# A fused embedding, attention and mixture-of-experts layer on one core: three experts in flight, all products on VectorE, routing weights folded in as square roots

## The chip, the core and the metric

The kernel runs on one core of one Trainium2 chip. The core has five engines with an instruction stream each: TensorE (PE), VectorE (DVE), ScalarE (ACT), GpSimd (POOL) and SyncE (SP, which only issues transfers). They wait for one another by semaphores. The metric is the device time of one execution in microseconds (us), as a median of several runs.

## What is computed

Token ids of shape 8 x 1024 pick rows of 256 numbers from a table. Then comes one layer, here cut to what matters:

```
h = table[x]                                         # 8 x 1024 x 256
n = layernorm(h)
q, k, v = n @ Wqkv + b          # 16 heads of 16; attention runs over the 8 rows of a column
h = h + softmax(q k^T / 4) v @ Wo + bo
n = layernorm(h)
s = sigmoid(n @ Wg)                                  # 16 experts in 4 groups
cw = top-4 experts within the 2 best groups, chosen by s + bias;  cw = 2.5 * s / sum(s)
h = h + relu(n @ Ws1)^2 @ Ws2 + sum_e cw[e] * relu(n @ W1[e])^2 @ W2[e]
```

## The kernel before

The 1024 columns are cut into B = 16 blocks of 64 columns, so a block has T = 512 tokens. All weights lie in SBUF as a high and a low part (`_hi`, `_lo`, the low part being what rounding to fp32r left over), and each product is three matmuls: high x high, high x low, low x high. So each activation that TensorE reads is also split in two: a rounded copy and a difference.

**The expert steps.** Each block has 18 steps (X_ALL): two halves of the shared expert and 16 routed experts. A step is `up` (6 matmuls of 512 columns into `psH`), an activation chain, and `down` (12 matmuls of 256 columns, added up in `psY`). The chain for a routed expert is: ScalarE takes relu of `psH` into `r_sb` (L497) and squares it (L499); VectorE multiplies by the broadcast routing weight `cwB` into `p_sb` (`weigh`, L641); ScalarE rounds `p_sb` to `hid_hi` (L510); VectorE subtracts to get `hid_lo` (`hidden_lo`, L647). `up` runs two experts ahead of `down`, and `psH`, `r_sb`, `p_sb` and `hid` have two buffers each. At the end of a block VectorE adds `psY` to `h` (`add_experts`, L653).

**The stages around them.** Attention, normalisation and routing of the following blocks are laid into these steps by tables of half steps h = 0 to 35. While block b's experts run, `attention(b+1, h)` and `head(b+2, h)` do one piece each at fixed h, before and after the expert's own instruction. `head` holds the first normalisation, its transposes (`k_sb` to `psB`), q, k and v, and the first product. `attention` holds the products q x k (`product`, L279, eight per block, four of them on GpSimd and four on VectorE, into the four slots of `ring`), their sum over heads by matmul (`score`, L940), softmax, spreading of the probabilities (L956), the weighted values on VectorE (L684, eight per block), their sums over positions (`position_sum`, L300 to L305, six on GpSimd and two on VectorE; the result goes to `q_sb`), the output projection (L966), second normalisation (`v_sb`), transposes, logits (L978), and the routing on VectorE (L707 to L758, five pieces). `rstd_of` on GpSimd gives 1/sqrt(variance) from the statistics of L659, and VectorE applies it (`normalise`, L666). The routing weights are transposed on TensorE, stored to DRAM and read back spread over all partitions (`cwB`).

**What sets the order.** Each engine runs its instructions in the order in which they stand; nothing is moved by a scheduler. Block 0's stages and part of block 1's run first, then a hardware loop runs seven times over two blocks, and the last two blocks stand in straight code. Weights are loaded and split in the meantime of block 0's stages.

## Time and profile before

| | |
|---|---|
| median of 3 runs | 1469.57 us (1466.58 to 1469.63) |
| span of the profiled execution | 1464.6 us |
| busy: TensorE, VectorE | 1267.7 us (87%), 1189.9 us (81%) |
| busy: GpSimd, ScalarE | 689.5 us (47%), 679.8 us (46%) |
| chain that ended last | VectorE 39%, TensorE 31%, issue 19%, others 11% |

The busy time of TensorE counts pipelined matmuls to their modelled ends, so a high share doesn't mean that it runs at its peak. The span is cut by the recurring work: VectorE's addition at L653 closes each of the 16 blocks, and the distance of two such rows is the time of a block in the middle of the run. "issue" in the chain is time for which the profile shows no wait.

### The profile page before, as it was taken

The page shows a single profiled execution, that of the slowest core. Times are in us where ns is not written, and L with a number is a line of the kernel's source. Part 1 is how long each engine was busy: PE and PEld are TensorE (multiplying, and loading weights), DVE is VectorE, ACT ScalarE, POOL GpSimd, SP SyncE. Part 2 cuts the span into 40 slices and gives each one's busy share as a digit, 9 for nine tenths or more (in the row PEclk, how much of TensorE's full clock was granted, in tenths as well). Part 3 has the DMA queues.
Part 4 walks back from the last instruction along what each step waited for, and adds up shares of the span by engine and source line. Part 5 has one row for each costly group of instructions (what it writes and reads, how often), then busy time and mean ns, then how long its engine had stood idle before and what let it go on. Part 6 is the DMA issues. An engine that isn't in the chain of part 4 may idle for free.

```text
span 1464.6 us, 22940 instructions
## 1 busy us (share of the span) xinstructions
PE 1267.7 (87%) x7488; PEld 1033.1 (71%) x7488; DVE 1189.9 (81%) x1792; ACT 679.8 (46%) x1138; POOL 689.5 (47%) x753
## 2 busy tenths in 40 slices
PE   4458898889888899888989889898988989989898
PEld 2146767768677687767778677776867768677787
DVE  3868889697987969789797888969798797978854
ACT  2234444544444454444544444454553445445355
POOL 7744535365263635535464363536526363442600
PEclk9579999999999999999999999999999999999999
DMA  2302111111211112111111212112121111212122
GB/s 66 125 16 74 58 60 58 61 62 55 73 62 57 58 44 88 58 61 58 66 65 44 78 67 62 58 46 73 58 73 58 61 58 44 88 44 73 59 73 73
DMA packets 33748, 92.21 MB, mean 63 GB/s; under 512 B 4800, under 2 KB 13376, under 8 KB 33600
## 3 DMA queue, kind: packets, MB, share of 16 engines
q1 hardware_dynamic: 30528, 81.99, 16.7%
q0 software_dynamic: 3072, 8.39, 2.0%
q8 instruction: 75, 1.23, 0.4%
q14 instruction: 73, 0.60, 0.1%
HBM read 81.46 MB, written 8.91 MB: 62 GB/s over the span
## 4 chain that ended last, share of the span: by engine, by line
DVE 39%; PE 31%; issue 19%; POOL 5%; ACT 5%; DMA 1%; DVEq 1%; ACTq 0%; POOLq 0%; SPq 0%
PE psY L900 9%; PE psH L887 8%; DVE ring L684 7%; PE psB L927 5%; DVE p_sb L641 5%; DVE hid_lo L647 5%; PE psA L966 3%; DVE g_gt L723 2%; DVE ring L300 2%; PE psA L978 2%; DVE ring L302 2%; DVE ring L279 1%; DVE k_sb L666 1%; ACT hid_hi L510 1%; DVE stats L659 1%
## 5 line engine op out<-in xcount | busy, mean ns | idle before, releaser
L900 PE MATMUL psY<-w_hi,hid_hi 128*128 128x256 f32 x1152 | 339.0, 294 | 53.6 <-DVE hid_lo L647 50.3
L510 ACT CAST hid_hi<-p_sb 128x512 fp32r<-128x512 f32 x256 | 159.2, 622 | 388.8 <-DVE p_sb L641 379.5
L900 PE MATMUL psY<-w_lo,hid_hi 128*128 128x256 f32 x1152 | 330.5, 287 | 0.0
L900 PE MATMUL psY<-w_hi,hid_lo 128*128 128x256 f32 x1152 | 330.2, 287 | 0.0
L279 POOL TENSOR_TENSOR ring<-q_sb,k_sb 128x1024 f32<-128x1024 f32 x64 | 169.1, 2653 | 309.1 <-PE psA L940 205.2
L900 PEld LDWEIGHTS psY<-w_hi,hid_hi 128*128 128x128 f32 x1152 | 223.6, 194 | 107.4 <-DVE hid_lo L647 72.6
L647 DVE TENSOR_TENSOR hid_lo<-p_sb,hid_hi 128x512 fp32r<-128x512 f32 x256 | 214.6, 838 | 93.4 <-ACT hid_hi L510 73.7
L887 PE MATMUL psH<-xT_hi,w_hi 128*128 128x512 f32 x576 | 235.6, 409 | 10.9 <-issue 8.7
L641 DVE TENSOR_TENSOR p_sb<-r_sb,cwB 128x512 f32<-128x512 f32 x256 | 214.2, 837 | 34.1 <-ACT r_sb L499 27.2
L900 PEld LDWEIGHTS psY<-w_lo,hid_hi 128*128 128x128 f32 x1152 | 224.6, 195 | 9.8
L887 PE MATMUL psH<-xT_lo,w_hi 128*128 128x512 f32 x576 | 230.2, 400 | 0.0
L887 PE MATMUL psH<-xT_hi,w_lo 128*128 128x512 f32 x576 | 229.8, 399 | 0.0
L900 PEld LDWEIGHTS psY<-w_hi,hid_lo 128*128 128x128 f32 x1152 | 224.6, 195 | 0.0
L300 POOL TENSOR_TENSOR ring<-ring 128x512 f32<-128x512 f32 x96 | 146.8, 1529 | 135.8 <-DVE ring L684 134.3
L497 ACT ACTIVATE r_sb<-psH 128x512 f32<-128x512 f32 x288 | 171.2, 594 | 57.2 <-PE psH L887 44.2
L499 ACT ACTIVATE r_sb<-r_sb 128x512 f32<-128x512 f32 x288 | 182.6, 634 | 9.1
L887 PEld LDWEIGHTS psH<-xT_hi,w_hi 128*128 128x128 f32 x576 | 111.0, 193 | 54.6 <-issue 23.1
L887 PEld LDWEIGHTS psH<-xT_hi,w_lo 128*128 128x128 f32 x576 | 109.9, 191 | 26.0
L887 PEld LDWEIGHTS psH<-xT_lo,w_hi 128*128 128x128 f32 x576 | 110.8, 192 | 16.9
L399 POOL TENSOR_TENSOR mv<-stats 128x4 f32<-128x4 f32 x32 | 20.3, 635 | 197.0 <-DVE stats L659 197.0
L302 POOL TENSOR_TENSOR ring<-ring 128x256 f32<-128x256 f32 x96 | 104.1, 1085 | 7.5
L279 DVE TENSOR_TENSOR ring<-q_sb,k_sb 128x1024 f32<-128x1024 f32 x64 | 89.6, 1401 | 21.5 <-issue 9.3
(133 smaller groups left out, 2137.5 us busy)
## 6 DMA issues: line engine op xcount, KB each, us to landing
cwB<-cw_dram SPq DMA_DIRECT2D x128, 512.0 KB, 3.7
out<-h SPq DMA_DIRECT2D x32, 256.0 KB, 5.4
p_sb<-w_t SPq DMA_DIRECT2D x3, 512.0 KB
cwB<-w_t SPq DMA_DIRECT2D x3, 512.0 KB, 4.5
h<-w_t SPq DMA_DIRECT2D x2, 512.0 KB
xin<-table,idx_now POOLq DMA_INDIRECT x56
cwB<-wqkv_t SPq DMA_DIRECT2D x2, 384.0 KB, 3.2
cw_dram<-cwT SPq DMA_DIRECT2D x16, 32.0 KB, 1.6
```

What stands on the lines that cost most here:

```text
L279: ns.tensor_tensor(ring[:, t % 4, :, :].rearrange("p l (m n) -> p l m n", m=L), qv.unsqueeze(2).to_broadcast([P, 2, L, NN]), kv.unsqueeze( ...
L300: ns.tensor_tensor(a[:, :, 0:4, :], a[:, :, 0:4, :], a[:, :, 4:8, :], ALU.add).then_inc(sum_step[who], 1)
L302: ns.tensor_tensor(a[:, :, 0:2, :], a[:, :, 0:2, :], a[:, :, 2:4, :], ALU.add).then_inc(sum_step[who], 1)
L497: nc.scalar.activation(r_sb[:, e % 2, :], psH[:, e % 2, :], ACT.Relu).then_inc(relu_done, 1)
L499: nc.scalar.activation(r_sb[:, e % 2, :], r_sb[:, e % 2, :], ACT.Square).then_inc(sq_done, 1)
L510: nc.scalar.copy(hid[0][:, e % 2, :], src[:, e % 2, :]).then_inc(hid_hi, 1)
L641: nc.vector.tensor_tensor(p_sb[:, e % 2, :], r_sb[:, e % 2, :], cwB[:, (r // QN) % 2, r % QN, :], ALU.mult).then_inc(p_ready, 1)
L647: nc.vector.tensor_tensor(hid[1][:, e % 2, :], src[:, e % 2, :], hid[0][:, e % 2, :].bitcast(f32), ALU.subtract).then_inc(hid_lo, 1)
L684: nc.vector.tensor_tensor(ring[:, t % 4, :, :], ps[:, :, :], v_sb[:, ih, :].unsqueeze(1).to_broadcast([P, 2, T]), ALU.mult).then_inc(av_re ...
L887: last = nc.tensor.matmul(psH[:, e % 2, :], W1[a][:, kh, e, :], x[b][:, kh, :], start=(kh == 0 and (a, b) == PASSES[0]), stop=(kh == KH - ...
L900: last = nc.tensor.matmul(psY[:, j // 2, (j % 2) * D:(j % 2 + 1) * D], hid[a][:, e % 2, j * P:(j + 1) * P], W2[b][:, e, :], start=(e == 0 ...
L927: last = nc.tensor.matmul(psB[:, n % 2, :], WQKV[a][:, kh, 2 * c + ih, :], xT1[b][:, kh, :], start=(kh == 0 and (a, b) == PASSES[0]), stop ...
```

## The change

- **Experts.** `up` runs three experts ahead (AHEAD), `hid` has three buffers (R). The routing weight is applied as its square root ahead of the square: VectorE does `max(psH, 0) * cwB` in one instruction from PSUM into `r_sb`, ScalarE squares twice, once as fp32 into `p_sb` and once rounded into `hid_hi`, VectorE subtracts. The shared halves keep the relu on ScalarE. `weigh` works two experts ahead of `down`'s step and `hidden_lo` one, so no engine needs another's result of the same step.
- **Products.** All eight are on VectorE.
- **Attention's output** goes to a tile of its own, `o_sb`; its split parts go to `xT2` in place of `xT1`, the second normalisation's result to `o_sb` in place of `v_sb`, and scores go to `psB` in place of `psA`.
- **Normalisation** is applied on ScalarE (identity with scale and bias from `rstd` and a new `nmr`, which GpSimd computes with one more operation).
- **Root of the weights.** ScalarE computes `exp(-0.5 * ln(1 + exp(-x)))`, GpSimd the power -0.5 of the sum; VectorE multiplies them. Loads of activation tables are placed when the program is built (the last order below shows them).
- **Order.** The stages of a block stand at positions p = 0 to 71 in one table. While block b's experts run, positions 36 to 71 of block b+1 and 0 to 35 of block b+2 are laid in. All products, scores and softmax and the first two weighted values now lie below 36. There is no hardware loop; everything stands in straight code, with constants in the waits.
- **Start.** Weights come in other pieces through eight staging areas; the first q, k, v matmuls wait for all of GpSimd's constants (`CONST_ALL`).

```
-        hid = [sb(f"hid_{p}", [P, 2, T], f32r) for p in ("hi", "lo")]
+        hid = [sb(f"hid_{p}", [P, R, T], f32r) for p in ("hi", "lo")]
...
-            def relu_square(blk, e):
...
-                nc.scalar.activation(r_sb[:, e % 2, :], psH[:, e % 2, :], ACT.Relu).then_inc(relu_done, 1)
-                nc.scalar.activation(r_sb[:, e % 2, :], r_sb[:, e % 2, :], ACT.Square).then_inc(sq_done, 1)
...
-            def hidden_hi(blk, e):
...
-                nc.scalar.copy(hid[0][:, e % 2, :], src[:, e % 2, :]).then_inc(hid_hi, 1)
...
+            def square(n):
...
+                if e < SH:
+                    nc.scalar.activation(r_sb[:, n % 2, :], psH[:, n % 2, :], ACT.Relu).then_inc(relu_done, 1)
...
+                nc.scalar.activation(p_sb[:, n % 2, :], r_sb[:, n % 2, :], ACT.Square)
+                wait(act, w2_mm, n - R + 1)
+                nc.scalar.activation(hid[0][:, n % R, :], r_sb[:, n % 2, :], ACT.Square).then_inc(hid_hi, 1)
...
-                nc.vector.tensor_tensor(p_sb[:, e % 2, :], r_sb[:, e % 2, :],
-                                        cwB[:, (r // QN) % 2, r % QN, :], ALU.mult).then_inc(p_ready, 1)
+                nc.vector.scalar_tensor_tensor(r_sb[:, n % 2, :], psH[:, n % 2, :], 0.0, cwB[:, (r // QN) % 2, r % QN, :],
+                                               ALU.max, ALU.mult).then_inc(weighed, 1)
...
+                    act.wait_ge(sigexp_ready, nth(blk, 1, 1))
+                    nc.scalar.activation(lgt[:, :, :], sig[:, :, :], ACT.Ln, bias=1.0).then_inc(log_ready, 1)
+                    act.wait_ge(log_ready, nth(blk, 1, 1))
+                    nc.scalar.activation(lgt[:, :, :], lgt[:, :, :], ACT.Exp, scale=-0.5).then_inc(root_ready, 1)
...
+            def root_of_sum(blk):
...
+                nc.gpsimd.tensor_tensor(w_rec[:, :], w_sum[:, :], half_neg[:, :], ALU.pow).then_inc(sum_root_ready, 1)
...
-            def main(blk, nxt, far):
-                for t in (5, 7):
-                    product(pool, nc.gpsimd, blk, t)
...
+        SCORES = [20, 23, 27, 29]
+        SPREADS = [34, 34, 36, 37, 39, 39, 41, 42]
+        V_PRODUCTS = [14, 16, 18, 19, 22, 22, 25, 27]
...
             def step_of(blk, e):
+                n = blk * X_ALL + e + AHEAD
+                if n < B * X_ALL:
+                    up(n)
+                stage_of(blk + 1, HALF + 2 * e)
+                stage_of(blk + 2, 2 * e)
+                down(blk, e)
+                stage_of(blk + 1, HALF + 2 * e + 1)
+                stage_of(blk + 2, 2 * e + 1)
```

The order on VectorE around the softmax, in a block in the middle of the run. Before (L641 is `weigh`, L647 `hidden_lo`, L684 a weighted value; REGISTER_ALU rows are the loop's arithmetic for waits):

```order
L772 TENSOR_TENSOR s_sb<-psA,s_max 128x512
L641 TENSOR_TENSOR p_sb<-r_sb,cwB 128x512
L777 TENSOR_REDUCE s_sum<-s_sb 128x64
...
L788 TENSOR_TENSOR probs<-s_sb,probs 64x512 x2
...
L666 TENSOR_SCALAR k_sb<-xin,mv,rstd 128x256 x4
L638 REGISTER_ALU
L641 TENSOR_TENSOR p_sb<-r_sb,cwB 128x512
L680 REGISTER_ALU
L684 TENSOR_TENSOR ring<-psB,v_sb 128x1024
```

The same place after (L663 is `hidden_lo`, L692 a weighted value):

```order
L789 TENSOR_REDUCE s_max<-psB 128x64
L792 TENSOR_TENSOR s_sb<-psB,s_max 128x512
L797 TENSOR_REDUCE s_sum<-s_sb 128x64
L799 RECIPROCAL s_rec<-s_sum 128x64
L801 TENSOR_TENSOR s_sb<-s_sb,s_rec 128x512
L663 TENSOR_TENSOR hid_lo<-p_sb,hid_hi 128x512 x2
L808 TENSOR_TENSOR probs<-s_sb,probs 64x512 x2
L692 TENSOR_TENSOR ring<-psB,v_sb 128x1024
L692 TENSOR_TENSOR ring<-psA,v_sb 128x1024
```

The `weigh` between the subtraction of the maximum and the sum is gone, and so are the normalisation and the `weigh` between the probabilities and the first weighted value.

The order on VectorE in the routing, after (L658 is `weigh`, L300 a product, L732 to L768 are routing):

```order
L727 TENSOR_REDUCE gsc<-pairs 128x16
L658 SCALAR_TENSOR_TENSOR r_sb<-psH,cwB 128x512
L663 TENSOR_TENSOR hid_lo<-p_sb,hid_hi 128x512
L732 TENSOR_TENSOR g_gt<-gsc 128x64
...
L736 TENSOR_REDUCE g_rank<-g_gt 128x16
L300 TENSOR_TENSOR ring<-q_sb,k_sb 128x1024 x2
...
L763 TENSOR_SCALAR w_sum<-w_sum 128x4
L766 TENSOR_TENSOR cw<-lgt,e_gt 128x64
L768 SCALAR_TENSOR_TENSOR cw<-cw,w_rec 128x64
L300 TENSOR_TENSOR ring<-q_sb,k_sb 128x1024
```

Products stand between the pieces of the routing, and between L763 and L768 lies the power on GpSimd that L768 waits for.

The order on ScalarE at the logits, after (L522 and L524 are the two squares, L593 copies the logits, L596 to L600 are the three functions):

```order
L593 COPY lg<-psA 128x128
L596 ACTIVATE sig<-lgt 128x64
L598 ACT_TABLE_LOAD
L598 ACTIVATE lgt<-sig 128x64
L600 ACT_TABLE_LOAD
L600 ACTIVATE lgt<-lgt 128x64
L522 ACTIVATE p_sb<-r_sb 128x512
L524 ACTIVATE hid_hi<-r_sb 128x512
```

Each block has two loads of activation tables ahead of the next expert's squares; before, the whole program has one, at its start.

## Rows read from the trace of the kernel before

**Rows 1.** Two blocks: us, then busy (count) of PE, PEld, DVE, ACT, POOL; clock, DMA

```profile
637.00:726.00 89.00, 79.88 (x471) 65.03 (x471) 74.28 (x112) 42.22 (x72) 42.94 (x46) 0.96 0.19 61
726.00:811.50 85.50, 77.33 (x467) 63.55 (x465) 73.58 (x113) 40.91 (x69) 42.71 (x46) 0.98 0.18 63
```

**Rows 2.** VectorE's timeline (start, duration), the additions that close blocks

```profile
200.60 1.22 DVE L653 TENSOR_TENSOR h<-psY,h 128x1024 f32<-128x1024 f32 x1
...
811.48 1.22 DVE L653 TENSOR_TENSOR h<-psY,h 128x1024 f32<-128x1024 f32 x1
...
1332.51 1.22 DVE L653 TENSOR_TENSOR h<-psY,h 128x1024 f32<-128x1024 f32 x1
...
1409.47 1.22 DVE L653 TENSOR_TENSOR h<-psY,h 128x1024 f32<-128x1024 f32 x1
...
1458.99 1.23 DVE L653 TENSOR_TENSOR h<-psY,h 128x1024 f32<-128x1024 f32 x1 [1.79 <-PE psY L900]
```

**Rows 3.** The chain that ended last, one block: start us, us, what

```profile
707.66 1.69 PE psA L978 x16
...
775.40 2.87 PE psA L966 x24
778.27 1.40 PE psH L887 x6
779.67 1.42 PE psY L900 x12
...
793.21 1.69 PE psA L978 x16
```

**Rows 4.** VectorE's timeline in the same block, wait ahead in brackets

```profile
712.82 1.87 DVE L641 TENSOR_TENSOR p_sb<-r_sb,cwB 128x512 f32<-128x512 f32 x1 [0.73 <-ACT r_sb L499]
714.61 2.42 DVE L723 TENSOR_TENSOR g_gt<-gsc 128x64 f32<-128x64 f32 x1
...
728.30 2.89 DVE L647 TENSOR_TENSOR hid_lo<-r_sb,hid_hi 128x512 fp32r<-128x512 f32 x1
...
733.61 2.11 DVE L647 TENSOR_TENSOR hid_lo<-p_sb,hid_hi 128x512 fp32r<-128x512 f32 x1 [0.69 <-ACT hid_hi L510]
...
748.51 0.69 DVE L641 TENSOR_TENSOR p_sb<-r_sb,cwB 128x512 f32<-128x512 f32 x1
749.11 1.22 DVE L684 TENSOR_TENSOR ring<-psB,v_sb 128x1024 f32<-128x1024 f32 x1
...
774.17 0.68 DVE L800 TENSOR_TENSOR xT_lo<-q_sb,xT_hi 128x512 fp32r<-128x512 f32 x1
```

**Rows 5.** GpSimd's timeline in the same block

```profile
711.74 5.21 POOL L279 TENSOR_TENSOR ring<-q_sb,k_sb 128x1024 f32<-128x1024 f32 x2 [6.59 <-ACT k_sb L528]
...
738.86 0.57 POOL L399 TENSOR_TENSOR mv<-stats 128x4 f32<-128x4 f32 x1 [3.68 <-DVE stats L659]
...
741.72 1.05 POOL L411 TENSOR_TENSOR rstd<-mv,half_neg 128x4 f32<-128x4 f32 x1
750.41 1.30 POOL L300 TENSOR_TENSOR ring<-ring 128x512 f32<-128x512 f32 x1 [7.65 <-DVE ring L684]
...
769.60 0.52 POOL L305 TENSOR_TENSOR q_sb<-ring 128x128 f32<-128x128 f32 x1
```

**Rows 6.** Groups by line and form: xcount, busy us, mean ns, idle before

```profile
L499 ACT ACTIVATE r_sb<-r_sb 128x512 f32<-128x512 f32 x288 | 182.6, 634 | 9.1
...
L491 ACT ACT_TABLE_LOAD x1 | 1.3, 1283 | 0.9 <-PEq L1084 0.9
...
L491 ACT CAST w_hi<-cwB 128x256 fp32r<-128x256 f32 x2 | 0.8, 404 | 0.0
```

**Rows 7.** Waits in the block of 89.0 us: total, times, longest

```profile
PEld psH L887 <- issue: 3.1, 2, 2.3
```

**Rows 8.** GpSimd's timeline at the start, its last constant

```profile
26.99 0.91 POOL L467 TENSOR_SCALAR_AFFINE_SELECT not_first<-not_first 128x64 f32<-128x64 f32 x1
```

**Rows 9.** The chain at the start: block 0's second transposed split

```profile
97.35 1.15 DVE xT_lo L673
```

More of the change, by code:

```diff
@@ L122, in lm_tower_layer @@
         rstd = [sb(f"rstd{w}", [P, TT]) for w in range(2)]
+        nmr = [sb(f"nmr{w}", [P, TT]) for w in range(2)]
         lg = sb("lg", [P, TT, 2, E])
@@ L160, in lm_tower_layer @@
         small_in = sem("small_in")
-        w_in = [sem(f"w_in{k}") for k in range(STAGES)]
+        w_in = [sem(f"w_in{k}") for k in range(14)]
         w_hi = sem("w_hi")
@@ new lines, in normalise @@
+            def normalise(w, blk, src, dst):
+                act.wait_ge(ln_rstd[w], nth(blk, 1, 1))
+                if w == 0:
+                    wait(act, prod_ready[1], nth(blk, LP, 0))
+                d = dst[:, :, :].rearrange("p a t -> p (a t)").rearrange("p (j d) -> p j d", d=D)
+                for j in range(TT):
+                    last = nc.scalar.activation(d[:, j, :], src[:, j, :], ACT.Identity,
+                                                bias=nmr[w][:, j:j + 1], scale=rstd[w][:, j:j + 1])
+                last.then_inc(xn_ready[w], 1)
@@ L613, in _ @@
-            with act.Fori(0, B // 2 - 1) as i:
-                block_act((i, 0), (i, 1), (i, 2))
-                block_act((i, 1), (i, 2), (i, 3))
-            block_act((None, B - 2), (None, B - 1), None)
-            block_act((None, B - 1), None, None)
+            for p in range(HALF):
+                stage_of(0, p)
+                if p == A_T1 + 2:
+                    act.wait_ge(const_step, CONST_ALL)
+                    nc.scalar.copy(spread[:, :, :].rearrange("p a b -> p (a b)"),
+                                   rows(r_sb[:, :, :])).then_inc(spread_ready, 1)
@@ L833, in block_dve @@
-            def block_dve(blk, att, nxt):
-                for e in range(X_ALL):
-                    if e + 1 < X_ALL:
-                        weigh(blk, e + 1)
-                    for h, last in ((2 * e, False), (2 * e + 1, True)):
-                        if att is not None:
-                            attention(att, h)
-                        if nxt is not None:
-                            head(nxt, h)
-                        if last:
-                            break
-                        if e + 1 < X_ALL:
-                            hidden_lo(blk, e + 1)
-                        elif att is not None:
-                            hidden_lo(att, 0)
-                add_experts(blk)
@@ L850, in _, with step_of @@
-            for h in range(V_T1):
-                head((None, 0), h)
-            for k in range(PIECES_QKV):
+            def step_of(blk, e):
+                n = blk * X_ALL + e
+                if n + 2 < B * X_ALL:
+                    weigh(n + 2)
+                if n + 1 < B * X_ALL:
+                    hidden_lo(n + 1)
+                if e == 0 and blk > 0:
+                    add_experts(blk - 1)
+                for k in range(PIECES_ATT, PIECES_ALL):
+                    if n == LO_AT[k - PIECES_ATT] - HALF:
+                        weight_lo(k)
+                for h in (2 * e, 2 * e + 1):
+                    stage_of(blk + 1, HALF + h)
+                    stage_of(blk + 2, h)
```

655 lines of the change are left out of this document (332 added, 323 removed).

## The prediction

> **What bounds the kernel now.** I read the shares of busy time first: TensorE 87%, VectorE 81%, both too high for either to be idle for long and too low for either to be the limit everywhere. So I cut the run into blocks. The additions that close a block stand 200.60 to 1332.51 us, 13 blocks apart [rows 2], 87.1 us each; the last but one takes 77.0 us (1332.51 to 1409.47) and the last 49.5. About 1208 of the 1465 us are blocks 1 to 14, so the block in the middle decides.
>
> In a block of 85.5 us TensorE is busy for 77.3 and VectorE for 73.6 [rows 1]. The chain tells which of them sets the time. From one logits' end (707.66 + 1.69 = 709.35) to the next (793.21 + 1.69 = 794.90) is 85.5 us [rows 3]. In its second part, from the start of the output projection at 775.40 to 794.90, the chain is TensorE without a gap: 19.5 us. In its first part, 709.35 to the end of the last split of attention's output at 774.17 + 0.68 = 774.85 [rows 4], it runs over VectorE: 65.5 us, and 0.55 to hand over. So the block is a ring of two parts: **65.5 us of VectorE, then 19.5 us of TensorE**. I split the first again at the end of the first weighted value (749.11 + 1.22 = 750.33) [rows 4]: 41.0 us of routing, products and softmax, and 24.5 us of weighted values and position sums. In the latter GpSimd works without a gap from 750.41 to 769.60 + 0.52 = 770.12 [rows 5].
>
> Two more things cost time. First, VectorE's instructions with both inputs in SBUF stretch whenever GpSimd runs: a subtraction that takes 0.69 takes 2.89 and 2.11, a comparison of 64 elements 2.42 [rows 4], in the shadow of a 2.6 us product [rows 5]; the ones from PSUM (L684, 1.22) do not. The Trainium skill's "SBUF — State Buffer", Who interferes with whom, says that the pair of ports shared by VectorE and GpSimd is an exclusive lock; by that rule, these rows agree. Second, the longer block (89.0 against 85.5 us, [rows 1]) has 3.1 us in which TensorE waited for nothing that is shown [rows 7], and 0.02 less clock. Blocks alternate in this way, so I take it as the edge of the loop, one per two blocks. The Trainium skill, "Runtime: NRT & Kernel Launch", Instruction fetch mechanics, says that a taken branch outside the fetched window costs a fetch; the row fits it, but does not show the fetch.
>
> **The first 41.0 us, term by term.** Start-to-start distances count, not durations: a `weigh` occupies VectorE for 749.11 - 748.51 = 0.60 us [rows 4].
> - GpSimd's products go: their shadow goes with them: 1.87 - 0.69, 2.42 - 0.22, 2.89 - 0.69 and 2.11 - 0.69 [rows 4] are 7.0 us less. This stretch had four products on VectorE, and has four after (positions 22, 22, 25, 27); the other four now lie at 14 to 19, in the part that TensorE fills. A product is 1.13 us start to start, as L684 with the same 1024 elements.
> - The normalisation of the next block moves to ScalarE: 1.3 us less (4 of 0.41, overlapped). There it costs 4 of 0.40 [rows 6].
> - Two waits for `hid_hi` within a step, 0.69 each [rows 4], go, since no step needs a result of its own: 1.4 less.
> - Two `weigh` and one `hidden_lo` fewer, 1.8 less. The block's closing addition and the first statistics now follow the first weighted value: 2.5 less here (and they lie beside GpSimd's sums there).
> - **Added:** the exponential is no longer covered by a `weigh`: 0.65 and two hand-overs, 0.8 more. Its cover was the instruction between L772 and L777.
> - The power on GpSimd takes 1.05 [rows 5] and replaces a reciprocal of 0.18, with hand-overs and one more product 1.2 more. Nothing covers it: behind the wait stand a product and two expert steps. GpSimd could be late there, but its queue holds only the bias addition ahead.
> - The probabilities' split is followed at once by the values that need them spread: 0.75 more (its cover was the normalisation).
> - **Two table loads per block**, 1.28 each [rows 6], with Ln and a second exponential: ScalarE stands for 3.3 us at the logits. The squares of one expert wait behind them, and VectorE's `hidden_lo` for them: in order, route part 1 takes VectorE 1.8 and the next `weigh` 0.6, so 5.4 - 3.4 = 2.0 us more.
>
> Sum: 41.0 - 7.0 - 1.3 - 1.4 - 1.8 - 2.5 + 0.8 + 1.2 + 0.75 + 2.0 = **31.7 us**; I take 31.
>
> `weigh` now reads PSUM, and no row has this form. Bounds: 0.60 as before, or below (a gain of 0.1) if its reads escape GpSimd as L684 does, to 0.7 if clamping costs something; by 11 of them 1 us at most. I take 0.60.
>
> **The 24.5 us of sums.** The sums stay six on GpSimd (19.7 us, [rows 5]) and two on VectorE. Now the next block's variance root stands between them in GpSimd's order, 738.86 to 742.77, 3.9 us [rows 5]. GpSimd then needs 23.6, and the copy and split of the output 1.5 more: 25.1. VectorE alone needs about the same: six steps of 1.2, seven values of 1.13, two sums of 1.95, closing addition and statistics 2.4, 21.4 in all, and up to 3 of locking. **25.1 us.** If the root were late, statistics of step 1 delay it and all sums behind it: up to 3 us more.
>
> **The TensorE part.** From projection to logits it now has all six q, k, v groups instead of three: 2.87 + 6 x 1.40 + up and down (1.40 and 1.42, three and two of them) + transposes 0.87 + logits 1.69 = **20.9 us** [rows 3]. VectorE and the root for the second normalisation fit beside it (2.7 + 4 + 1.3 of 12.7 us).
>
> Block: 31 + 25.1 + 0.5 + 20.9 = **77.5 us**, and no loop edge. TensorE's own work is the same: 77.3 us busy, of which ends of matmuls that waited are part; I put it at 74 to 76. So TensorE is about to be the limit as well.
>
> ScalarE, at 42 us of 85.5 [rows 1], loses one 0.63 operation [rows 6] for each of 16 experts and gains 1.3 x 2 + 3.1: 37.
>
> **Start and end.** Block 0's chain: q, k, v now wait for GpSimd's last constant at 26.99 + 0.91 = 27.9 [rows 8] and not 20.6, 7 us later; its eight products on VectorE win that back (9 against 16 us), and eight staging areas some 3 us: the transposed split ends at 95 in place of 97.35 + 1.15 = 98.5 [rows 9]. Then logits 3.5 and the 31 us stretch, with 11 expert instructions less (-6.6), five weight splits (+5.6) and the second value: the first period starts at about **127 us**. Fourteen full periods follow, then a block without the head of another: 77.5 less q, k, v, transposes and scores (14.2) is **63.3**. The last: 18 `down` and 15 `up` (46.6), the closing addition 1.2 and 5.6 to the span's end: **53.4**, as before's last block already runs at TensorE's pace.
>
> Sum: 127 + 14 x 77.5 + 63.3 + 53.4 = 1328.7 us of span. The median before lies 5.0 above the span shown (1469.57 - 1464.6), so **1334 us**.
>
> **The rivals.**
> - *TensorE is the limit.* If the sums on GpSimd and the waits of ScalarE are covered, a block is TensorE's own 75.5: 14 x 2 less, **1306 us**. For it: two engines within 3 us of each other. Against: TensorE has to wait for the split output once a block.
> - *The table load costs more than its row.* The one row (1.28) stands at the start, with nothing ahead of it. If ScalarE must also run empty, a switch costs about double, VectorE's `hidden_lo` waits 2.7 longer: 14 x 2.7, **1372 us**. The Trainium skill, "ScalarE: Activation LUTs", What ACT_TABLE_LOAD costs, has 1283 ns and a drain of 1380 ns. By its section Table sets one set holds both exp and ln; the built order has two loads a block all the same, so that rule gives nothing here.
> - *The sums stretch.* GpSimd and VectorE each have 22 to 25 us there, and lock one another out; 5 us more a block, **1404 us**. For it: in the same stretch before, subtractions already stretch.
> - *Slower than before.* VectorE is in order, and each of its waits then stops the expert chain: q, k, v at position 16 (3.2), the transposes at 55 (2), tables 2, exponential, power and spreading 2.7, beside its own 71 and 8 of locking, is 88.9 us. It decides from 87.3 us a block on. 14 x 11.4 more: **1494 us**. Against: half of these waits lie in the part that TensorE fills.
>
> **How the numbers follow.** Forecast 0.50 (1320 to 1355 on its own), TensorE as the limit 0.16, tables 0.11, sums 0.16, slower 0.05; the remaining 0.02 no change. The range for 8 in 10 goes from the one rival to the other, 1300 to 1405. 0.2% is about what a measurement of this kernel can tell from no change: faster 0.93, same 0.02, slower 0.05.
>
> **What would show it.** Closing additions 77 to 78 us apart and all alike, without alternation; no stretched comparison in the routing; on ScalarE two table loads of 1.28 a block with one `hidden_lo` waiting about 2 us; TensorE waiting 2 to 3 us a block at the output projection; a first closing addition at about 206 us. I am wrong if the blocks still alternate, if a `weigh` from PSUM takes clearly more than 0.7, or if GpSimd's sums take more than 25 us from the first value.

## The result and the profile after

The changed kernel takes **1339.39 us** (median of 4 runs, 1338.98 to 1341.05); the kernel before, on the same chip, 1469.6 (1466.58 to 1470.88). The ratio is 0.9124, 95% interval 0.9103 to 0.9145. The prediction was 1334 us (1300 to 1405), faster.

The page after: TensorE's share of busy time has risen from 87% to 92%, VectorE's is 80% (81% before), ScalarE's 47% (46%), GpSimd's 39% (47%).

```profile
PE 1228.9 (92%) x7488; PEld 1020.1 (76%) x7488; DVE 1067.7 (80%) x1726; ACT 630.1 (47%) x1072; POOL 524.8 (39%) x723
...
DVE 45%; PE 28%; ACT 10%; issue 10%; POOL 4%; DVEq 2%; DMA 1%; ACTq 0%; POOLq 0%; SPq 0%
```

The second line is the chain that ended last, by engine. It gives VectorE 45%, and it misleads, as will be seen. VectorE's timeline has the additions that close blocks (L669 now), and answers to [rows 2]:

```profile
215.26 1.21 DVE L669 TENSOR_TENSOR h<-psY,h 128x1024 f32<-128x1024 f32 x1
...
602.54 1.21 DVE L669 TENSOR_TENSOR h<-psY,h 128x1024 f32<-128x1024 f32 x1
...
680.01 1.21 DVE L669 TENSOR_TENSOR h<-psY,h 128x1024 f32<-128x1024 f32 x1
...
1222.36 1.21 DVE L669 TENSOR_TENSOR h<-psY,h 128x1024 f32<-128x1024 f32 x1
1287.14 1.23 DVE L669 TENSOR_TENSOR h<-psY,h 128x1024 f32<-128x1024 f32 x1
1333.90 1.22 DVE L669 TENSOR_TENSOR h<-psY,h 128x1024 f32<-128x1024 f32 x1 [2.90 <-PE psY L905]
```

The first and the fourteenth are 13 blocks and 1007.1 us apart: 77.47 a block, where [rows 2] give 87.1. The one shown is 77.47 too; the alternation of [rows 1] is gone. One block in the windows view, whole and in two parts (columns as in [rows 1]):

```profile
602.54:680.01 77.47, 75.28 (x468) 62.98 (x468) 65.76 (x108) 38.32 (x67) 32.38 (x45) 1.00 0.22 69
...
626.23:667.87 41.64, 41.64 (x265) 33.75 (x265) 32.23 (x65) 21.04 (x38) 12.60 (x16) 1.00 0.16 51
667.87:703.70 35.83, 33.65 (x206) 29.24 (x205) 33.53 (x44) 17.29 (x31) 19.79 (x28) 1.00 0.27 90
```

The first part goes from the output projection to the end of the last scores. **TensorE is busy for all of its 41.64 us.** In the second, up to the next projection, it waits 2.2 us, in three places:

```profile
PE psY L905 <- DVE h L669: 1.5, 1, 1.5
PE psA L973 <- DVE xT_lo L820: 0.4, 1, 0.4
PE psB L963 <- DVE probs L808: 0.3, 1, 0.3
```

So a change to another engine can save TensorE 2.2 us of waiting a block, and little else. (It isn't a strict bound: busy time counts matmuls to their modelled ends, and a later run took 0.44 us off it as well.) The granted clock has changed too: it is 1.00 here, and was 0.96 and 0.98 in [rows 1], where about the same matmuls were busy for 79.88 and 77.33 us in place of 75.28. VectorE at the logits, in the same block (start, duration; it answers to the first rows of [rows 4]):

```profile
650.30 0.69 DVE L658 SCALAR_TENSOR_TENSOR r_sb<-psH,cwB 128x512 f32<-128x512 f32 x1 [0.29 <-PE psH L890]
652.42 0.69 DVE L663 TENSOR_TENSOR hid_lo<-p_sb,hid_hi 128x512 fp32r<-128x512 f32 x1 [1.42 <-ACT hid_hi L524]
653.03 0.22 DVE L732 TENSOR_TENSOR g_gt<-gsc 128x64 f32<-128x64 f32 x1
...
664.29 0.23 DVE L768 SCALAR_TENSOR_TENSOR cw<-cw,w_rec 128x64 f32<-128x64 f32 x1 [1.09 <-POOL w_rec L444]
...
668.08 0.68 DVE L789 TENSOR_REDUCE s_max<-psB 128x64 f32<-128x512 f32 x1
```

The comparison of 64 elements is back from 2.42 to 0.22. The two waits which the prediction charged to the block, for the table loads (1.42) and for the power (1.09), are there in size. The scores end at 667.87 on TensorE, and VectorE takes them up at 668.08: both engines arrive within 0.2 us of each other. What these waits cost is therefore open in this trace, and the first experiments test it.

### The profile page after: what moved, and what is told of

The parts are those of the page before. It is cut to its first block, busy times and chain, and to the rows that moved or that the text cites. A ratio compares the mean times of both kernels' runs of the same rounds, so it can differ in the third digit from the quotient of the medians.

```text
span 1339.3 us, 19873 instructions
## 1 busy us (share of the span) xinstructions
PE 1228.9 (92%) x7488; PEld 1020.1 (76%) x7488; DVE 1067.7 (80%) x1726; ACT 630.1 (47%) x1072; POOL 524.8 (39%) x723
## 4 chain that ended last, share of the span: by engine, by line
DVE 45%; PE 28%; ACT 10%; issue 10%; POOL 4%; DVEq 2%; DMA 1%; ACTq 0%; POOLq 0%; SPq 0%
DVE hid_lo L663 10%; PE psB L932 8%; DVE ring L692 7%; PE psY L905 7%; PE psH L890 6%; DVE r_sb L658 6%; DVE ring L300 4%; PE psA L973 4%; DVEq L741 2%; DVE ring L320 2%; ACT p_sb L522 2%; DVE o_sb L327 2%; DVE stats L675 2%; ACT hid_hi L524 2%; ACT L598 1%
## 5 line engine op out<-in xcount | busy, mean ns | idle before, releaser
L522 ACT ACTIVATE p_sb<-r_sb 128x512 f32<-128x512 f32 x288 | 180.9, 628 | 346.8 <-DVE r_sb L658 345.7
L663 DVE TENSOR_TENSOR hid_lo<-p_sb,hid_hi 128x512 fp32r<-128x512 f32 x288 | 232.7, 812 | 27.2 <-ACT hid_hi L524 26.8
L320 POOL TENSOR_TENSOR ring<-ring 128x512 f32<-128x512 f32 x96 | 126.6, 1318 | 239.6 <-DVE ring L692 239.6
L300 DVE TENSOR_TENSOR ring<-q_sb,k_sb 128x1024 f32<-128x1024 f32 x128 | 160.0, 1263 | 70.1 <-ACT k_sb L552 69.6
L658 DVE SCALAR_TENSOR_TENSOR r_sb<-psH,cwB 128x512 f32<-128x512 f32 x256 | 174.2, 681 | 30.7 <-PE psH L890 30.6
L524 ACT ACTIVATE hid_hi<-r_sb 128x512 fp32r<-128x512 f32 x288 | 178.2, 619 | 9.5 <-PE psY L905 8.5
L444 POOL TENSOR_TENSOR w_rec<-w_sum,half_neg 128x4 f32<-128x4 f32 x16 | 16.6, 1040 | 289.8 <-DVE w_sum L763 289.8
L692 DVE TENSOR_TENSOR ring<-psB,v_sb 128x1024 f32<-128x1024 f32 x64 | 77.7, 1214 | 14.3 <-PE psB L963 14.3
L932 PE MATMUL psB<-xT_hi,wqkv_hi 128*128 128x512 f32 x192 | 79.3, 413 | 8.0 <-POOL not_first L493 8.0
L322 POOL TENSOR_TENSOR ring<-ring 128x256 f32<-128x256 f32 x96 | 81.9, 853 | 7.5
```

What stands on the lines that cost most here:

```text
L300: ns.tensor_tensor(ring[:, t % 4, :, :].rearrange("p l (m n) -> p l m n", m=L), qv.unsqueeze(2).to_broadcast([P, 2, L, NN]), kv.unsqueeze( ...
L320: ns.tensor_tensor(a[:, :, 0:4, :], a[:, :, 0:4, :], a[:, :, 4:8, :], ALU.add).then_inc(sum_step[who], 1)
L322: ns.tensor_tensor(a[:, :, 0:2, :], a[:, :, 0:2, :], a[:, :, 2:4, :], ALU.add).then_inc(sum_step[who], 1)
L522: nc.scalar.activation(p_sb[:, n % 2, :], r_sb[:, n % 2, :], ACT.Square)
L524: nc.scalar.activation(hid[0][:, n % R, :], r_sb[:, n % 2, :], ACT.Square).then_inc(hid_hi, 1)
L658: nc.vector.scalar_tensor_tensor(r_sb[:, n % 2, :], psH[:, n % 2, :], 0.0, cwB[:, (r // QN) % 2, r % QN, :], ALU.max, ALU.mult).then_inc(w ...
```

## The experiments

Each changed kernel ran in four executions beside the kernel before (1467.5 to 1469.7 us in the four sets). The median is a blunt measure for edits of a few microseconds, since the last block but one comes out in different lengths. In it TensorE waits 3.2 us for `o_sb`, and what follows runs for a longer or a shorter while at the lower level of its clock. Here is that block in the changed kernel and in one of the kernels below (the one with both moves and the later wait; windows):

```profile
1222.36:1287.14 64.78, 60.09 (x381) 54.18 (x382) 46.50 (x87) 29.81 (x53) 19.05 (x27) 0.97 0.22 74
```

```profile
1200.72:1269.48 68.76, 64.15 (x381) 57.91 (x382) 46.49 (x87) 30.25 (x53) 19.06 (x27) 0.90 0.22 70
```

The same 381 matmuls take 4.1 us more at a granted clock of 0.90. The block is 68.6 to 68.9 us long in the profiled executions without the logarithm, with the early statistics, with the early root and with both moves, 67.2 with the power covered, and 64.5 to 65.6 in those with the later wait alone and with the addition in halves. So the distance of closing additions in the middle is the measure of an edit, and up to 4 us of a median are not the edit's.

### The logarithm and its table loads, left out

```
-                    nc.scalar.activation(lgt[:, :, :], sig[:, :, :], ACT.Ln, bias=1.0).then_inc(log_ready, 1)
+                    nc.scalar.activation(lgt[:, :, :], sig[:, :, :], ACT.Identity).then_inc(log_ready, 1)
```

> The changed kernel with the logarithm replaced by an identity, which leaves out part of the computation: the routing weights are then not the root of the sigmoid. Both table loads of each block go with it. Theory: the loads cost what hid_lo waits behind them in the trace, 1.4 us a block, up to the 2.0 us of my sum: 14 to 16 blocks, 1309 to 1319 us. Rival A (each load also drains the engine): 4 us or more a block, below 1285 us. Rival B (TensorE is the limit already and takes the gain): within 5 us of 1339.

Measured: 1341.17 us (1340.26 to 1342.07), ratio 0.9128. VectorE there, at the same places:

```profile
647.24 0.68 DVE L663 TENSOR_TENSOR hid_lo<-p_sb,hid_hi 128x512 fp32r<-128x512 f32 x1
...
664.30 0.69 DVE L789 TENSOR_REDUCE s_max<-psB 128x64 f32<-128x512 f32 x1 [1.25 <-PE psB L945]
```

The wait of 1.42 is gone, and one of 1.25 for the scores has come 17 us later. Blocks take 77.36 us, 0.1 less. (The profiled execution begins 3.2 us sooner and loses 3.8 in the last block but one.) **The loads cost nothing where they stand**, since TensorE has the time of that stretch.

### The wait for the power, covered

```
-        ROUTE_FIRST = [0, 1, 8, 13, 16, 21, 27]
+        ROUTE_FIRST = [0, 1, 8, 13, 16, 21, 26, 27]
...
-        V_ROUTE = [56, 57, 58, 61, 63, 63]
+        V_ROUTE = [56, 57, 58, 61, 63, 63, 64]
```

> The changed kernel, with the last operation of the routing (the one that waits about 1.1 us a block for the power on GpSimd) one half step later, so that a product and an expert step stand in between; nothing else is moved. The prediction charged this wait to every block (1.2 us, nothing covers it). Theory A: it is on the path, and 1.1 us a block come off: 1322 to 1326 us. Theory B: it lies where TensorE is the limit (output projection to the last scores), VectorE's wait for the last scores grows by as much, and nothing moves: 1336 to 1342 us.

Measured: 1339.62 us (1337.56 to 1342.14). The wait is gone from the row, and the same trade appears:

```profile
661.83 0.22 DVE L769 SCALAR_TENSOR_TENSOR cw<-cw,w_rec 128x64 f32<-128x64 f32 x1
664.24 0.69 DVE L790 TENSOR_REDUCE s_max<-psB 128x64 f32<-128x512 f32 x1 [0.99 <-PE psB L946]
```

A block takes 77.37 us, again 0.1 less, and theory B holds. Together the two show that in the routing stretch, 31 us in the prediction, taking away one of VectorE's waits buys nothing. It doesn't follow that adding to it is free, which the next run tests.

### Products on GpSimd again

```
+                for t in (1, 3, 5, 7):
+                    if p == V_PRODUCTS[t]:
+                        product(pool, nc.gpsimd, blk, t)
...
-                    if p == V_PRODUCTS[t]:
+                    if p == V_PRODUCTS[t] and t % 2 == 0:
```

> The changed kernel, with products 1, 3, 5 and 7 (positions 16, 19, 22 and 27) on GpSimd again, as before; the tables and all else stay. It undoes the one part to which the prediction gave its largest term, 7.0 us a block. Theory A, the prediction's own: a block's routing stretch is VectorE's, so four shadows of GpSimd stretch its subtractions and comparisons again, less four products of 1.13 that it no longer does: 7.0 - 4.5 = 2.5 to 7 us a block, and a product of 2.6 instead of 1.13 ahead of the last scores 1.5 more. By 14 to 15 blocks: 1380 to 1440 us. Theory B, from the run without the logarithm: from the output projection to the last scores TensorE is the limit (41.7 us of a block) and VectorE has about 1.3 us to spare at the end of it, so most of this is covered: 0 to 2 us a block, 1340 to 1370 us.

Measured: 1394.17 us (1391.4 to 1395.4), 55 more than the changed kernel. That is theory A's range, not B's. A block takes 80.48 us, 3.0 more, and 11 us come once, at the start (first closing addition at 226.08; the edit also lets GpSimd wait there until the weights are split, since `ring` holds them). GpSimd and VectorE at the same moment:

```profile
682.86 2.41 POOL L300 TENSOR_TENSOR ring<-q_sb,k_sb 128x1024 f32<-128x1024 f32 x1 [3.00 <-PE psB L949]
685.22 2.86 POOL L439 TENSOR_TENSOR xin<-xin,bo_sb 128x1024 f32<-128x1024 f32 x1
```

```profile
683.22 2.60 DVE L667 TENSOR_TENSOR hid_lo<-p_sb,hid_hi 128x512 fp32r<-128x512 f32 x1
685.74 2.42 DVE L743 SCALAR_TENSOR_TENSOR cho<-g_rank,cho 128x64 f32<-128x64 f32 x1
```

A subtraction that takes 0.68 alone ends 0.55 us after GpSimd's product, and an operation of 0.22 ends 0.08 us after GpSimd's bias addition. That addition was there before; in the changed kernel it runs at 643.06, ahead of the routing, and the products in front of it in GpSimd's order push it into the routing. VectorE is busy 67.06 us a block in place of 65.76 though it has four products fewer: 1.3 + 4 x 1.13 = 5.8 us of stretching. VectorE had no slack against this in the changed kernel, where it took up the scores 0.2 us after they were there, and 3.0 us reach the end of the block. They are seen on TensorE: its waits in the block are 4.9 us in place of 2.2, the new ones for `weigh` (1.2), for the routing weights (1.0) and for the probabilities (0.8 in place of 0.3). So TensorE isn't busy for all of the first part any more. This is the largest part of the change that a single run isolates.

### From the other side: the old kernel without its loop, then without GpSimd's products

The loop written out on all engines:

```
-            with pe.Fori(0, B // 2 - 1) as i:
+            for i in range(B // 2 - 1):
```

> The kernel before, with its seven passes of the hardware loop written out as straight code; nothing else differs. My theory: the alternation of block lengths (89.0 and 85.5 us) is the loop's edge, 2 to 3.5 us each, so 7 edges go: 1446 to 1456 us, ratio to before 0.984 to 0.990, and all blocks in the middle near 85.5 us. Rival: the alternation comes from something else with a period of two blocks (buffers alternate too), and the time stays at 1470 us with blocks that still alternate.

Measured: 1445.3 us (1442.35 to 1447.97), ratio 0.9839 (0.9789 to 0.9888). Two blocks far apart are now alike (windows view):

```profile
200.86:286.01 85.15, 77.81 (x470) 64.17 (x469) 73.37 (x112) 41.39 (x71) 42.73 (x46) 0.98 0.20 63
626.62:711.77 85.15, 77.91 (x470) 64.24 (x469) 73.37 (x113) 41.40 (x71) 42.73 (x46) 0.98 0.20 63
```

The loop's seven passes cost 23.5 us, 3.4 each (16 to 31 us by the interval, 2.4 to 4.4 a pass). Then, on top of it, the odd products on VectorE, behind the even ones:

```
-                for t in (5, 7):
-                    product(pool, nc.gpsimd, blk, t)
...
+                    product(dve, nc.vector, blk, 2 * V_PRODUCTS.index(h) + 1)
```

> The kernel before in straight code, and all eight products on VectorE, each odd one right behind the even one before it. To be compared with the same kernel without that move. My theory, by the terms of the sum: GpSimd's lock takes 7.0 us a block from VectorE's part of the ring, and four more products of 1.13 us add 4.5 there: 2.5 us less a block, some 37 us less in 15 blocks, 1410 to 1420 us. Rival: VectorE is the engine that decides and only gets more work: 4.5 us more a block, 1515 us.

Measured: 1421.96 us (1419.09 to 1424.21), 23 less than with the loop written out alone. The direction is right, the size a miss, and the trace tells where: the first closing addition comes at 189.35 in place of 200.86, and a block is 84.29 instead of 85.15. So 11.5 us are won once at the start and only 0.9 a block. The block, to be held against the two above:

```profile
612.23:696.52 84.29, 77.86 (x470) 64.19 (x469) 71.00 (x116) 41.30 (x71) 32.15 (x42) 0.98 0.20 63
```

VectorE is busy 2.4 us less (71.00 for 73.37), close to the 7.0 - 4.5 = 2.5 that the shadows less four products of 1.13 give, and the block is shorter by 0.9. The waits say where the rest went. TensorE's wait for the routing weights fell from 1.2 to 0.2 us, while its waits for `hid_lo` (3.1, now 3.2) and for the values (2.5) stayed. VectorE for its part now waits 3.1 us for ScalarE's `r_sb` in place of 1.3.

### Two experts in flight in the new order

```
-    R = 3
-    AHEAD = 3
+    R = 2
+    AHEAD = 2
...
-            up(2)
```

> The changed kernel with two experts in flight instead of three (R and AHEAD 2); the order of all other work is the same. My sum had no term for the depth as such, only for the waits within a step that go. Theory: with two, the second square of an expert waits for down of the expert before the last, so VectorE can't run ahead of TensorE; where it does now, it waits: 2 to 5 us more a block, 1370 to 1415 us. Rival: the depth is not what brought the gain (the order is), and the time stays within 5 us of 1339.

Measured: 1705.68 us (1704.54 to 1707.24), ratio 1.1608. A clear miss, by over 290 us. One block is 102.35 us (windows), and the waits in it say why:

```profile
645.75:748.10 102.35, 84.62 (x468) 69.05 (x468) 64.01 (x109) 39.33 (x67) 31.89 (x45) 0.92 0.16 52
```

```profile
DVE r_sb L658 <- PE psH L890: 32.4, 10, 9.1
...
ACT hid_hi L524 <- PE psY L905: 18.9, 5, 8.6
...
PE psA L985 <- DVE xT_lo L681: 3.7, 1, 3.7
```

`weigh` works two experts ahead, and with two in flight that is the expert whose `up` TensorE has in hand in the same step. VectorE waits 32.4 us a block for it, its products and splits queue up behind, and TensorE waits for those (the last row is the longest of its waits; it is idle for 17.7 us of the block). The wait that was expected, the second square behind `down`, is there too (18.9 us on ScalarE); the one for `up` wasn't foreseen. The new order is only good with `up` three ahead. The edit takes away the lead and the third `hid` buffer together, so what each is worth is open, and so is what they would be worth in the old order, which had two of both with its steps dealt out otherwise; that was not run.

### The start

```
-                if p == A_T1 + 2:
+                if p == A_QKV[-1] + 1:
...
-            pe.wait_ge(const_step, CONST_ALL)
...
+                if p == SCORES[0]:
+                    pe.wait_ge(const_step, CONST_ALL)
```

> The changed kernel, with TensorE's wait for all of GpSimd's constants ahead of the first scores (position 20) instead of the first q, k, v, and the copy of one of these constants on ScalarE behind q, k, v of block 0. It tests what the start costs, once. q, k, v of block 0 start at 32.04 us in the changed kernel, the constants end at 31.95, while the split of the normalised rows is there some us earlier. If this wait is what delays the start, the first closing addition comes 4 to 10 us earlier (205 to 211 in place of 215.26) and the time is 1329 to 1335 us. If the loads of weights through eight staging areas set the start (the rows of block 0 land at 13 instead of 9 us, the weights after them), less than 3 us: 1336 to 1340. Blocks stay at 77.4 us in both.

Measured: 1335.13 us (1333.38 to 1336.63), 4.3 less. q, k, v of block 0 begin at 26.50 us and not at 32.04. The first addition stands at 208.01, but kernels whose start is unchanged have it at 215.26, 211.98 and 212.10, so by the traces 4 to 7 us can be the effect; the medians and the run with both moves below give 4 to 5.

### The stretch of the sums

First the statistics of the next block's first normalisation, from behind the first value to position 21 of the block before:

```
-                if p == V_STATS1:
-                    dve.wait_ge(xin_in[par], 64 * (blk // 2 + 1))
-                    norm_stats(0, blk, xin[par])
+                for at, nb in ((V_STATS1, 0), (21, blk + 1)):
+                    if p == at and nb < B and (p == 21 or blk == 0):
+                        dve.wait_ge(xin_in[nb % 2], 64 * (nb // 2 + 1))
+                        norm_stats(0, nb, xin[nb % 2])
```

> The changed kernel, with the first statistics of the next block (two instructions on VectorE, 1.3 us in all, from the same rows of x) at position 21 of the block before, among the products, instead of behind the first weighted value; the variance root on GpSimd stays where it was, between the position sums. Theory B: a block is a ring of TensorE from the output projection to the last scores (41.7 us) and VectorE from there to the output's split (35.8 us). 1.3 us of VectorE leave the second part, but GpSimd, which the root and six sums keep busy there, sets its end as well: the gain is 0 to 1.3 us a block, 1320 to 1339 us. If GpSimd's queue alone sets that part, nothing moves: 1338 to 1341.

Measured: 1330.75 us (1328.04 to 1333.36); 76.57 us a block, 0.9 less. TensorE's busy time in a block falls by 0.44 of it (75.28 to 74.84), and of its waits the 0.4 us at the output projection is gone. Thirteen blocks would give 11.7 us; the median fell by 8.6, since the last block but one is 4.1 longer. Then GpSimd's root as well:

```
-                if p == P_RSTD1 and blk > 0:
-                    rstd_of(0, blk)
+                if p == 28 and blk + 1 < B:
+                    rstd_of(0, blk + 1)
```

> The changed kernel, with both the first statistics (position 21 of the block before, VectorE) and the variance root that follows from them (position 28 of the block before, GpSimd, 4 operations, 3.9 us) moved ahead of the softmax. It takes 3.9 us of GpSimd and 1.3 us of VectorE out of the stretch of the sums, which the prediction made 25.1 us long because of GpSimd (19.7 for the sums, 3.9 for the root, 1.5 for the copy and split). The prediction's step: that stretch becomes 19.7 + 1.5 = 21.2 by GpSimd, but VectorE needs some 22.5 itself, so 1.3 to 2.6 us a block come off: 1303 to 1321 us. Rival: VectorE alone sets the stretch, and the gain is that of the statistics, as in the run with these alone. Lower bound of any such change: TensorE's own 75.3 us busy in a block of 77.4, so 2.1 us a block, 1308 us.

Measured: 1327.11 us (1326.47 to 1328.58); a block of 76.51 us, and the first addition at 209.63 rather than 214.39. That is above the expected 1303 to 1321. Taking 3.9 us off GpSimd gave 0.06 us a block; taking 1.3 off VectorE gave 0.9. The two blocks (windows), statistics alone and then with the root:

```profile
597.13:673.70 76.57, 74.84 (x468) 62.91 (x468) 65.39 (x109) 38.39 (x67) 31.97 (x45) 1.00 0.22 70
```

```profile
592.19:668.70 76.51, 74.81 (x468) 62.90 (x468) 65.38 (x108) 38.25 (x67) 32.14 (x45) 1.00 0.22 70
```

and the chain of the latter, by engine:

```profile
PE 56%; DVE 25%; issue 6%; ACT 6%; POOL 4%; DVEq 2%; DMA 1%; ACTq 0%; POOLq 0%; SPq 0%
```

The second run can't prove by itself that GpSimd was not the limit before, because with the statistics moved there was little left to gain. The trace of the changed kernel does: GpSimd's last sum there,

```profile
699.06 0.46 POOL L327 TENSOR_TENSOR o_sb<-ring 128x128 f32<-128x128 f32 x1
```

ends at 699.52, 4.1 us before the last split of the output does, and VectorE has no wait for GpSimd between the scores and that split. GpSimd did stretch VectorE's subtractions there, but its own queue was not the limit of that stretch. VectorE was, and after 0.9 us TensorE is. The chain has turned from VectorE 45% to TensorE 56%. In this kernel TensorE has one wait left worth the name, 1.5 us for the closing addition.

### Both, and the closing addition in halves

Both moves together with the later wait at the start:

> The changed kernel, with the two moves that shorten a block (first statistics at position 21, variance root at position 28 of the block before) and the later wait for GpSimd's constants at the start. If both effects are separate, a block stays at 76.5 us and the first closing addition comes 5 to 7 us earlier than 209.6: 1319 to 1323 us. If the earlier start is given back, since the weights' pieces come no sooner and TensorE catches up with them: 1324 to 1328 us.

Measured: 1322.25 us (1322.11 to 1323.39); blocks of 76.5, first addition at 205.55, 4.1 earlier than with the root moved alone. The effects add up. Then the addition in two halves, so that TensorE's first `down` of the next block waits for one of them:

```
-                nc.vector.tensor_tensor(h1[par][:, :, :].rearrange("p j d -> p (j d)"),
-                                        psY[:, :, :].rearrange("p a t -> p (a t)"),
-                                        h1[par][:, :, :].rearrange("p j d -> p (j d)"), ALU.add).then_inc(y_added, 1)
+                for a in range(2):
+                    half = h1[par][:, 2 * a:2 * a + 2, :].rearrange("p j d -> p (j d)")
+                    nc.vector.tensor_tensor(half, psY[:, a, :], half, ALU.add).then_inc(y_added, 1)
...
+                    if e == 0 and j == 2:
+                        pe.wait_ge(y_added, nth(blk, 2, 2))
```

> As the kernel with both moves and the later wait, and the closing addition of a block is cut into two halves of 512 elements each, so that TensorE begins the next block's first down when the first half is done. It tests that TensorE is the limit now: in the kernel with the root moved, TensorE waits 1.5 us a block for this addition, and VectorE's two moves gave the same 76.5 us a block with and without the root. If TensorE is the limit, half of the addition (0.6 us a block) comes off, 14 to 15 times: 1310 to 1315 us. If VectorE or GpSimd is, nothing or a little loss from one more instruction: 1320 to 1325 us.

Measured: **1313.83 us** (1312.5 to 1317.73), ratio 0.8949 (0.8917 to 0.8981), the best of all kernels here that compute the whole. Its block (windows) and TensorE's wait in it:

```profile
584.58:660.58 76.00, 74.83 (x468) 62.90 (x468) 65.52 (x109) 38.20 (x67) 33.18 (x45) 1.00 0.22 71
```

```profile
PE psY L908 <- DVE h L671: 1.0, 1, 1.0
PE psB L966 <- DVE probs L809: 0.2, 1, 0.2
```

The wait fell from 1.5 to 1.0 and the block by the same 0.5 us. Thirteen blocks make 6.5 us of it; the profiled execution is 10.9 shorter, because the last block but one is back at 65.60 us (3.2 less, clock 0.97) and the start is 1.0 earlier. So the median in the expected range is in part luck; the block isn't. 74.83 + 1.0 + 0.2 = 76.0: TensorE's work and its waits are the whole block. Last, the logarithm left out here as well (the same edit as in the first experiment):

> The kernel with both moves, the later wait and the halved addition, and with the logarithm left out (an identity stands in its place, so the routing weights are not those of the reference); the two table loads of a block go with it. In the changed kernel itself this left the block at 77.4 us. If TensorE is the limit of a block of 76.0 us all round, nothing moves here either: 1311 to 1316 us. If the VectorE stretch from the logits on, through the two loads, still sets a part of the block (the chain of that kernel is only 50% TensorE), up to the 1.4 to 2.0 us a block for which hidden_lo waits come off: 1286 to 1300 us.

Measured: 1312.43 us (1312.14 to 1314.02), blocks of 75.97. Nothing moves, though the chain of the kernel with halves was only 50% TensorE.

## Why the prediction was right, point by point

**The ring.** A block was predicted as 31 + 25.1 + 0.5 + 20.9 = 77.5 us and is 77.47. The parts of the block shown: the projection begins at 626.23, ScalarE takes the logits at 647.34 (21.1); the first value ends at 676.13 + 1.22 = 677.35 (30.0); the last split of the output ends at 702.95 + 0.69 = 703.64 (26.3), and TensorE goes on at 703.70 (0.06). Each part is within 1.2 us of its term. The rows (ScalarE, then VectorE):

```profile
647.34 0.27 ACT L593 COPY lg<-psA 128x128 f32<-128x128 f32 x1 [1.37 <-PE psA L985]
```

```profile
676.13 1.22 DVE L692 TENSOR_TENSOR ring<-psB,v_sb 128x1024 f32<-128x1024 f32 x1 [0.82 <-PE psB L963]
...
702.95 0.69 DVE L820 TENSOR_TENSOR xT_lo<-o_sb,xT_hi 128x512 fp32r<-128x512 f32 x1 [0.24 <-ACT xT_hi L585]
```

**But not for the reason given.** The terms of the routing stretch were added up as if VectorE alone set it. Taking away two of them, +2.0 for the table loads and +1.2 for the power, changed the block by 0.1 each. The same engine then waited 1.25 or 0.99 for the scores. The stretch is 30 us long because TensorE needs from 647 to 667.87 for its own work there, and VectorE, with the gains summed in the prediction, happens to need the same. That the block came out at 77.47 against 77.5 is luck to that extent. The working has two soft places as well: the sum of the stretch gave 31.7 and 31 was taken without a reason (10 us over 14 blocks), and of the two waits of 0.69 the rows show one (the trace has 0.63 for the other, at 725.42). The step that failed is the split of the ring: the TensorE part doesn't end at the logits, it ends at the last scores, 41.64 us of a block and not 20.9. The rival "TensorE is the limit" (75.5 a block) was put at 0.16 as a case by itself; it was true for over half of the block, and in the rest TensorE waited 2.2 us.

**The signs.** The blocks are alike, no comparison in the routing is stretched, and the two loads take 1.28 us each, as foretold; `hidden_lo` waits 1.42 rather than about 2. Two signs missed. TensorE was to wait 2 to 3 us at the output projection; it waits 0.4 there, and 1.5 for the closing addition, a wait that the prediction doesn't have. And the first closing addition stands at 215.26, not 206.

**TensorE's own work.** The 74 to 76 us are right (75.28), but the prediction put the fall from 77.3 down to the ends of matmuls that waited. The rows show a higher clock besides: the old kernel without its loop has 77.9 us at a granted clock of 0.98, the changed one 75.3 at 1.00. By these rows 1.6 of the 2.6 us are the clock's (an estimate: 0.02 of 77.9), and no term of the prediction has it.

**GpSimd's shadow** (7.0 us, the largest term) is real: 5.8 us of stretching come back with four products on GpSimd, the bias addition that they push back included. What it is worth depends on what waits behind: 3.0 us a block in the new order, 0.9 in the old.

**The loop's edge.** The prediction took the alternation of [rows 1] for it. The kernel before with the loop written out has 85.15 us in both kinds of block and is 23.5 us faster. That it is the loop is shown; whether its arithmetic for waits or the fetching of code costs the time is not. The 3.1 us of [rows 7] are the weight loads' wait; the matmuls show 2.1 there.

**The sums.** Predicted 25.1, measured 26.3, and the reason was wrong: GpSimd's 23.6 + 1.5 did not set it. GpSimd took 22.1 us from its first sum to its last, 0.9 of them waiting for VectorE. With the root gone from GpSimd's queue a block lost 0.06 us; with 1.3 us gone from VectorE, 0.9.

**Table loads** have their row's length and no more; the rival with the drain (1372 us) is out. **`weigh` from PSUM** takes 0.68, 0.60 from start to start, as assumed.

**Start and end.** The fourteenth addition was to stand at 127 + 14 x 77.5 = 1212 us and stands at 1222.36. That is all from the start. GpSimd's constants end not at 27.9 but at 31.94, since the rows of block 0 come later now, and GpSimd's work on them stands ahead of the constants. The first statistics, before and after:

```profile
9.83 1.41 DVE L659 BATCH_NORM_STATS2 stats<-xin 128x6 f32<-128x256 f32 x4 [9.83 <-DMA xin<-table,idx]
```

```profile
13.28 1.41 DVE L675 BATCH_NORM_STATS2 stats<-xin 128x6 f32<-128x256 f32 x4 [13.28 <-DMA xin<-table,idx]
...
31.67 0.27 POOL L493 TENSOR_SCALAR_AFFINE_SELECT not_first<-not_first 128x64 f32<-128x64 f32 x1
```

The run with the later wait shows a second part: with GpSimd's constants out of the way, q, k, v start at 26.50, when the split of the transposed rows is there, and not at 20.58 as before. The prediction gave the eight staging areas 3 us of gain and overlooked that their transfers are issued ahead of these rows' landing; that they are what delays the rows was not tried alone. The later wait for the constants gives 4 us back; the rest of the 10 is not settled.

The last block but one is 64.8 (63.3), the last, up to the span's end at 1339.3, is 52.2 (53.4). The offset of 5.0 us from span to median was wrong: the profiled run took 1341.05 us by the clock for 1339.3 us of span, and the median is 0.1 above the span of this, the slowest of the four. Fourteenth addition +10.4, last two blocks +0.2, offset -4.9: 5.7 us above the sum of 1333.7, which was rounded to 1334. Two errors of 10 and 5 us that nearly half cancel are luck too.

**Where the 130 us came from.** The loop 23.5. GpSimd's products 23 in the old order (1445.3 to 1421.96) or 55 in the new one (1394.17 to 1339.39). The rest, 52 to 83 us, is what the new order, the third expert in flight and the moved work do together; these weren't separated, and the run with two in flight shows that the new order needs its depth. What the higher clock gives is contained in these parts.

## What to carry to other kernels

Before costing an engine's instructions one by one, take the windows of the stretch and look whether another engine is busy for 100% of it. Here its neighbours' waits were then free, however they looked in the chain. The sum of the busiest engine's own waits in a block (2.2 us here, of which 1.5 were won) tells about what changes elsewhere can give. When two chains are within some tenths of a microsecond, a gain on one buys nothing, while a loss on it still costs: 5.8 us of stretching on VectorE cost 3.0. And a median moves for reasons of its own (4 us by the clock of one block here), so compare blocks.

## What the runs showed of the hardware

Two activation tables loaded one behind the other on ScalarE, with the functions between them (timeline of the changed kernel):

```profile
647.94 0.26 ACT L596 ACTIVATE sig<-lgt 128x64 f32<-128x64 f32 x1 [0.34 <-DVE lgt L716]
648.22 1.28 ACT L598 ACT_TABLE_LOAD   x1
649.51 0.26 ACT L598 ACTIVATE lgt<-sig 128x64 f32<-128x64 f32 x1
649.78 1.28 ACT L600 ACT_TABLE_LOAD   x1
651.08 0.26 ACT L600 ACTIVATE lgt<-lgt 128x64 f32<-128x64 f32 x1
```

A switch costs its 1.28 us: the load follows 0.02 us behind the function and the next function 0.01 behind the load. The drain that the Trainium skill gives in "ScalarE: Activation LUTs", What ACT_TABLE_LOAD costs, on top of 1283 ns doesn't show in these rows.

`weigh`, with one input in PSUM and one in SBUF, is not stretched beside GpSimd's sums, while the subtraction behind it is. GpSimd and VectorE in the block shown:

```profile
602.90 1.26 POOL L320 TENSOR_TENSOR ring<-ring 128x512 f32<-128x512 f32 x1
```

```profile
603.67 0.68 DVE L658 SCALAR_TENSOR_TENSOR r_sb<-psH,cwB 128x512 f32<-128x512 f32 x1
604.27 1.25 DVE L663 TENSOR_TENSOR hid_lo<-p_sb,hid_hi 128x512 fp32r<-128x512 f32 x1
```

Nor does every subtraction with both inputs in SBUF stretch when GpSimd works, as the prediction has it: the one at 687.09 takes 0.68, and it is GpSimd's small operation beginning at 687.20 that takes 0.65 in place of the 0.22 it takes at 632.72, when VectorE is idle.

A loop's pass cost 3.4 us by the medians (2.4 to 4.4 by the interval).

With two experts in flight the granted clock in the block shown is 0.92, where the changed kernel has 1.00, and the same 468 matmuls take 84.62 us of busy time in place of 75.28, which is 9.3 of the 24.9 us by which the block is longer. TensorE's timeline shows one place, behind a wait of 3.3 us:

```profile
692.97 1.33 PE L920 MATMUL psA<-ident,o_sb 128*128 128x128 f32 x8 [3.26 <-ACT o_sb L532]
...
694.53 0.63 PE L932 MATMUL psB<-xT_lo,wqkv_hi 128*128 128x512 f32 x1
...
697.09 0.40 PE L890 MATMUL psH<-xT_lo,w_hi 128*128 128x512 f32 x1
```

A matmul of 512 columns takes 0.63 us there and 0.40 again from 697.09 on, and the granted clock from 692.97 to 697.09 is 0.59. So part of the 366 us of that run is the lower of the clock's two levels (1.2 instead of 2.4 GHz), not waiting as such. The last block but one shows the same behind its wait of 3.2 us.
